# Keeping the running sums of the dense pairs in PSUM, in a four-layer graph network kernel

## The reference, cut to what matters

```
z  = relu(batchnorm2(y2))            # the end of layer 1
x2 = x1 + z                          # residual of layer 1
h  = relu(layernorm(x2))
x3 = x2 + (h after the six steps of layer 2)
g  = relu(layernorm(x3))
out = x3 + tanh(g' @ W1 + b1) @ W2 + b2   # layer 3; likewise without neighbours
```

## Time and profile before

| What | Value |
|---|---|
| median of three runs | 3728.46 us |
| span of the profiled execution, which is its own time here | 3778.5 us |
| PE busy | 2654.6 us, 70% |
| VectorE (DVE) busy | 2151.6 us, 57% |
| ScalarE (ACT) busy | 2009.2 us, 53% |
| GpSimd (POOL) busy | 1431.0 us, 38% |
| mean granted TensorE clock | 0.826 |

### The profile page before, as it was taken

The page is one execution under the profiler, slowest core; times in us unless marked ns, Lnnn a source line. Parts: engine busy times, 40 slices in busy tenths (PEclk is TensorE's granted clock), DMA queues, the critical chain, the costliest instruction groups (busy, mean ns, idle before and its releaser), DMA issues. The chain is left out here.

```text
span 3778.5 us, 45814 instructions
## 1 busy us (share of the span) xinstructions
PE 2654.6 (70%) x11055; PEld 1615.7 (43%) x11055; DVE 2151.6 (57%) x7980; ACT 2009.2 (53%) x4381; POOL 1431.0 (38%) x1507
## 2 busy tenths in 40 slices
PE   4666555656666667799999747787787878775641
PEld 2433333434544545554444322454454545443420
DVE  5533254556658856433333466677677777776620
ACT  1555455556556665455555488565666566553400
POOL 5444434442534335100000000546464645444476
PEclk8877777778888888999999858888889888876865
DMA  4544343344445555334334388444454444333210
GB/s 87 148 132 125 103 119 100 95 121 124 123 128 177 165 150 168 123 133 137 135 136 136 128 259 291 136 144 143 133 160 137 152 143 153 120 106 101 82 58 37
DMA packets 528965, 504.90 MB, mean 134 GB/s; under 512 B 58706, under 2 KB 389955, under 8 KB 528616
## 3 DMA queue, kind: packets, MB, share of 16 engines
q1 hardware_dynamic: 477388, 415.73, 34.4%
q0 software_dynamic: 47184, 85.73, 8.7%
q10 hardware_dynamic: 4172, 0.99, 0.1%
HBM read 246.45 MB, written 260.27 MB: 134 GB/s over the span
## 5 line engine op out<-in xcount | busy, mean ns | idle before, releaser
L1839 POOL DMA_INDIRECT h_G<-step_tab,row_i x294 | 282.0, 959 | 470.3 <-DMA step_tab<-l_NR 194.1
L796 PE MATMUL a_PA<-a_H,w 128*128 128x512 f32 x504 | 308.6, 745 | 197.7 <-ACT a_H L960 160.8
L1839 POOL DMA_INDIRECT h_M<-step_tab,row_i x294 | 283.8, 965 | 227.1 <-PE h_P L1944 148.0
L1559 DVE TENSOR_SCALAR b_Y<-b_BP,col 128x512 f32<-128x512 f32 x148 | 109.9, 743 | 354.2 <-PE b_BP L1513 354.2
L1513 PE MATMUL b_BP<-b_Z,w 128*128 128x512 f32 x592 | 266.3, 592 | 0.0
L270 POOL DMA_INDIRECT h_G<-msg_tab,row_i x147 | 142.1, 967 | 318.4 <-PE h_P L306 150.8
L1541 ACT ACTIVATE b_Z<-b_BQ,bn 128x512 f32<-128x512 f32 x148 | 115.0, 777 | 257.2 <-PE b_BQ L1505 256.9
L208 ACT ACTIVATE l_ln_sd<-l_ln_mv,lneps 128x8 f32<-128x8 f32 (+1 forms) x136 | 41.0, 301 | 383.1 <-DVE l_ln_mv L2149 219.6
L2185 DVE TENSOR_TENSOR_SCAN h_T<-keep,h_T,h_P 128x512 f32<-128x512 bf16 x196 | 223.3, 1139 | 35.7 <-issue 18.6
L796 PEld LDWEIGHTS a_PA<-a_H,w 128*128 128x128 f32 x504 | 105.9, 236 | 322.1 <-ACT a_H L960 191.5
L969 ACT ACTIVATE a_H<-a_PA,col 128x512 f32<-128x512 f32 x252 | 163.7, 669 | 140.0 <-PE a_PA L796 87.8
(11 more groups left out here) (384 smaller groups left out, 6730.5 us busy)
## 6 DMA issues: line engine op xcount, KB each, us to landing
b_HI<-hin_tab SPq DMA_DIRECT2D x148, 256.0 KB, 2.8
y_tab<-b_Y SPq DMA_DIRECT2D x148, 256.0 KB, 2.0
l_Y<-y_tab SPq DMA_DIRECT2D x148, 256.0 KB
l_X<-x_tab SPq DMA_DIRECT2D x148, 256.0 KB
x_tab<-a_X SPq DMA_DIRECT2D x112, 256.0 KB
hin_tab<-a_HI SPq DMA_DIRECT2D x112, 256.0 KB
a_XR<-in_x SPq DMA_DIRECT2D x97, 256.0 KB
out_rows<-l_O SPq DMA_DIRECT2D x97, 256.0 KB
```

What stands on the lines that cost most here:

```text
L796: nc.tensor.matmul(PA[b][:, 0:nt * P], w[:, :], h[b][:, 0:nt, :].rearrange("p t d -> p (t d)"), start=True, stop=True).then_inc(done, 1)
L1559: nc.vector.tensor_scalar(Y[b][:, :], BP[b][:, :], col[:, C_B12:C_B12 + 1], None, ALU.add).then_inc(b_y, 1)
L1839: pool.indirect_dma_start(out=GR_[i % 2][b][:, k, :], out_offset=None, in_=table[:, :], in_offset=bass.IndirectOffsetOnAxis(ap=row_i[:, t ...
```

## The change

For dense pairs the sum stays in the bank XB from the first transpose to the output. `turn` opens the group there with its transposes; a new `add_x1` has PE multiply the loaded x1 rows with the identity matrix onto the transposed z, in one 128x512 float32 matmul for each of the two groups; `x3` and `rows` no longer clear the bank, so r6, h, b2 and the last product land on top. Both layer norms of a dense pair, statistics on DVE and application on ACT, now read the bank. DVE's two adds of a group (in `x2` and `stats2`) are gone, and `rows_out` is a copy. SP's load of the x1 rows two pairs later waits for PE's `add_x1` in place of DVE's add. Edge pairs are as before.

```diff
@@ SP, load_x1
-                        after(sp, x2_set, 2 * (j - 2) + b + 1)
+                        if j >= 2:
+                            sp.wait_ge(*x2_done(j - 2, b))
@@ PE, turn
-                        last = nc.tensor.transpose(turned_in(j, b)[:, k * P:(k + 1) * P], Y[j % 2][b][:, k, :], ident[:, :])
+                        if is_d(j):
+                            last = nc.tensor.matmul(XB[j % 2][b][:, k * P:(k + 1) * P], Y[j % 2][b][:, k, :], ident[:, :], start=(k == 0),
+                                                    stop=(k == 3), is_transpose=True)
+                        else:
+                            last = nc.tensor.transpose(turned_in(j, b)[:, k * P:(k + 1) * P], Y[j % 2][b][:, k, :], ident[:, :])
+            def add_x1(j):
+                for b in range(2):
+                    pe.wait_ge(x1_in[j % 2][b], 16 * (j // 2 + 1))
+                    nc.tensor.matmul(XB[j % 2][b][:, :], ident[:, :], X1[j % 2][b][:, :, :].rearrange("p t d -> p (t d)"), start=False,
+                                     stop=True, skip_group_check=True).then_inc(x2_bank, 1)
@@ PE, the slots
                     turn(j)
+                    if is_d(j):
+                        add_x1(j)
@@ ACT, norm1 and norm2
-                        ln1.act_apply(act, j, b, X2[j % 2][b], NR[j % 2][b])
+                        ln1.act_apply(act, j, b, rows2(j, b), NR[j % 2][b])
-                        rows = X2[j % 2][b][:, k, :] if is_d(j) else XB[j % 2][b][:, k * D:(k + 1) * D]
+                        rows = XB[j % 2][b][:, k * D:(k + 1) * D]
@@ DVE, x2
+                    if is_d(j):
+                        continue
                 for b in range(2):
-                    dve.wait_ge(x2_set, 2 * j + b + 1)
+                    dve.wait_ge(*x2_done(j, b))
@@ DVE, stats2
-                    if is_d(j):
-                        nc.vector.tensor_tensor(X2[j % 2][b][:, :, :], X2[j % 2][b][:, :, :],
-                                                XB[j % 2][b][:, :].rearrange("p (t d) -> p t d", d=D), ALU.add).then_inc(x3_set, 1)
-                for b in range(2):
-                    if is_d(j):
-                        dve.wait_ge(x3_set, 2 * (j - D0) + b + 1)
@@ DVE, rows_out
-                    nc.vector.tensor_tensor(O[b][:, :, :], X2[r][b][:, :, :], XB[r][b][:, :].rearrange("p (t d) -> p t d", d=D),
-                                            ALU.add).then_inc(o_set, 1)
+                    nc.vector.tensor_copy(O[b][:, :, :].rearrange("p t d -> p (t d)"), XB[r][b][:, :]).then_inc(o_set, 1)
```

More of the change, by code:

```diff
@@ L1688, in build @@
     y_in, x1_in = ([sems(f"{n}{r}_", 2) for r in range(2)] for n in ("y_in", "x1_in"))
-    z_set, turned, x2_set, x3_sum, turned2, h_set, p1_set, tanh_set, p2_set, o_set, x3_set = (sem(n) for n in (
-        "z_set", "turned", "x2_set", "x3_sum", "turned2", "ht_set", "p1_set", "tanh_set", "p2_set", "o_set", "x3_set"))
+    z_set, turned, x2_set, x3_sum, turned2, h_set, p1_set, tanh_set, p2_set, o_set, x2_bank = (sem(n) for n in (
+        "z_set", "turned", "x2_set", "x3_sum", "turned2", "ht_set", "p1_set", "tanh_set", "p2_set", "o_set", "x2_bank"))
     normed2 = sems("normed2_", 2)
@@ L1705, in o_stores, with x2_done @@
         return 16 * no2(j, b)
+    def x2_done(j, b):
+        return (x2_bank, 2 * (j - D0) + b + 1) if is_d(j) else (x2_set, 2 * j + b + 1)
     def rows2(j, b):
+        if is_d(j):
+            return _Bank(XB[j % 2][b])
         return X2[j % 2][b] if full(j, b) else _Rows(XS, 4 * group(j, b))
@@ L1903, in x3 @@
                             pe.wait_ge(normed2[b], no2(j - 2, b) + 1)
-                        nc.tensor.matmul(XB[r][b][:, :], ones3[:, :], split_r6[:, :], start=True, stop=False)
+                        nc.tensor.matmul(XB[r][b][:, :], ones3[:, :], split_r6[:, :], start=not is_d(j), stop=False, skip_group_check=is_d(j))
                         if not is_d(j):
@@ L1907, in x3 @@
                         nc.tensor.matmul(XB[r][b][:, :], ident[:, :], NR[r][b][:, :, :].rearrange("p t d -> p (t d)"), start=False,
-                                         stop=True).then_inc(x3_sum, 1)
+                                         stop=True, skip_group_check=is_d(j)).then_inc(x3_sum, 1)
             def turn2(j):
@@ L1928, in rows @@
                     pc_user[b] = (tanh_set, n + 1)
-                    nc.tensor.matmul(XB[j % 2][b][:, :], ones3[:, :], split_out[:, :], start=True, stop=False)
+                    nc.tensor.matmul(XB[j % 2][b][:, :], ones3[:, :], split_out[:, :], start=False, stop=False, skip_group_check=True)
                     for k in range(4):
-                        last = nc.tensor.matmul(XB[j % 2][b][:, k * P:(k + 1) * P], HT[b][:, k, :], w32[:, :], start=False, stop=(k == 3))
+                        last = nc.tensor.matmul(XB[j % 2][b][:, k * P:(k + 1) * P], HT[b][:, k, :], w32[:, :], start=False, stop=(k == 3), skip_group_check=True)
                     last.then_inc(p2_set, 1)
@@ L2115, in x2 @@
                     if full(j, b):
-                        if j >= 2 and is_d(j - 2):
-                            dve.wait_ge(o_set, 2 * (j - 2 - D0) + b + 1)
-                        elif j >= 2 and full(j - 2, b):
+                        if j >= 2 and full(j - 2, b):
                             dve.wait_ge(x3_sum, no2(j - 2, 0) + no2(j - 2, 1) + (b + 1 if j - 2 > MIX else 1))
@@ L2135, in stats2 @@
                         dve.wait_ge(x3_sum, no2(j, 0) + no2(j, 1) + (b + 1 if j > MIX else 1))
-                    if is_d(j):
-                        nc.vector.tensor_tensor(X2[j % 2][b][:, :, :], X2[j % 2][b][:, :, :],
-                                                XB[j % 2][b][:, :].rearrange("p (t d) -> p t d", d=D), ALU.add).then_inc(x3_set, 1)
-                for b in range(2):
-                    if is_d(j):
-                        dve.wait_ge(x3_set, 2 * (j - D0) + b + 1)
                     for k in range(4):
-                        rows = X2[j % 2][b][:, k, :] if is_d(j) else XB[j % 2][b if full(j, b) else 0][:, k * D:(k + 1) * D]
+                        rows = XB[j % 2][b if full(j, b) else 0][:, k * D:(k + 1) * D]
                         last = nc.vector.bn_stats(ln2.st[:, 4 * b + k, :], rows)
@@ L2295, in build, with __init__, __getitem__ @@
     top.close()
+class _Bank:
+    def __init__(self, bank):
+        self.bank = bank
+    def __getitem__(self, at):
+        parts, j, cols = at
+        return self.bank[parts, j * D:(j + 1) * D]
 class _Rows:
```

## The result

The changed kernel takes 3670.27 us (median of 4 runs, 3661.72 to 3683.13), the kernel before 3726.86 (4 runs): a ratio of 0.9848, with a 95% interval of 0.982 to 0.9876. That is 57 us less, where the forecast was 35 (3693 us, range 3668 to 3742); the time is that of the rival "all of it reaches POOL's floor" (3671 us), and outside the forecast's own range of 3676 to 3711.

The account below looks back on a forecast made before the run. The loop through PE, DVE and ACT was taken to bound about half the slots, POOL's round the rest. Slots 18 + boundaries 12 + sixth step and last hops 8 - first pair 2 = 36 us, scaled to 3693 us, range 3668 to 3742.

Parts of the forecast that it names:

- all of it reaches POOL's floor: Rival: filling PE's gap raises its clock, POOL's h_M waits fall to 2.06 us; 58 us gained, 3671 us, chance 0.12.
- DVE's adds are on the path, PE's hole is filled: Slot loop: removing stats2's adds brings statistics, affine and norm2 1.18 us earlier; add_x1 uses PE's 1.84 us wait.
- the clock: PE in the steps: filling its gap may raise PEclk from 0.89, cutting a 3.62 us product to 2.2; only a rival.
- The fill costs 0.2 us a slot and is otherwise free: add_x1 between z's transposes and h_G: 2.2 us of matmuls on PE, h_G turned only 0.2 us later.
- The slots give 18 us, half of them at the floor: Whole steps: 12 of 24 h_M waits above POOL's 2.06 us gain 1.2 us each, 3.6 a step, 18 in five.
- first pair: First dense pair, without a hop or known idle PE to hide add_x1: 2.2 us lost.
- x2's adds are covered by the product, I count them at nothing: DVE's adds in x2, 1.28 us a pair, end before a scan PE needs only after its product; counted as no gain.
- The 8 us given to it: Sixth step and last hops: POOL caps nothing, seven dense pairs remain, six or seven times 1.2 us, 8 us gained.
- Boundaries, 2.4 us each: Between steps, from last h_M batch to next first gather: loop's 1.2 us plus stats2's 1.18, five boundaries, 12 us.
- Statistics and norm from the bank cost nothing: BN_STATS takes 284 ns from PSUM against 280 from SBUF; 32 per pair cost 0.1 us more, counted as nothing.
- The copy: rows_out on DVE as a copy from PSUM: at most 0.1 us a pair longer; taken at the replaced add's time.
- Slower: Rival: add_x1 at low clock takes 3.62 us, above the 3.0 us threshold; 27 us slower, 3755 us, chance 0.17.

Follow-up runs that it names:

- no_add2: Kernel before, with DVE's two adds in stats2 left out for dense pairs and no added PE work: 3233.03 us, ratio 0.9879.
- fill_only: Kernel before plus two float32 identity matmuls per dense pair ahead of z's transposes, results overwritten, DVE's adds kept: 3253.74 us, ratio 0.9943.
- the fourth group: Runs where the kernel before takes 3274 us: changed kernel 3163.3 us, without add_x1's matmuls 3162.98, with a third gather buffer 3154.96.
- after_2: The changed kernel run again, unaltered, in a later group of runs: 3732.7 us, ratio 0.9893 to the kernel before.
- the third group: Runs where the kernel before takes 3774 us, holding the changed kernel again (3732.7 us) and the kernel before without x2's adds (3752.39 us).
- no_add1: Kernel before with DVE's two adds in x2 left out for dense pairs, stats2's adds kept, no added PE work: 3752.39 us, ratio 0.9944.
- fill_double: Changed kernel plus two more identity matmuls per dense pair ahead of z's transposes, results overwritten: 3742.45 us, ratio 0.991 to the kernel before.
- x2_in_x3: Kernel before, x2's adds kept on DVE, stats2's adds replaced by two PE matmuls per pair in x3, behind h_M's turn: 3853.44 us, ratio 1.0222.

## Why the prediction was right, and where its terms were off

**DVE's adds are on the path, PE's hole is filled: right.** The loop named in the prediction (stats2, affine, h_G, norm2) is what got shorter: 43.7 us of idle time ahead of h_G became 2.4, and 66.6 ahead of l_NR became 22.6, while 37.5 came back ahead of the product. no_add2 shows the adds' part, fill_only the filling's, both in the group where the kernel takes 3274 us. The number is partly luck: two terms set at nothing, x2's adds and the clock, were too low, and the measured time lies in the range because that was drawn to take in the rival at 3671.

**The fill costs 0.2 us a slot and is otherwise free: right, and a little too dear.** add_x1 took 1.88 us, not 2.2, and in the fourth group it costs 0.2 us a slot by the two profiles and nothing in the whole kernel. PE's busy time was to rise by 110 us; with the better clock it went from 2654.6 to 2650.7.

**"The slots give 18 us, half of them at the floor": too small.** Of the 24 waits ahead of h_M, 9 stood within 0.2 us of the floor, 14 at 2.5 to 4.1 and one at 6.77; a gain of 1.2 us a slot could take 16 us of the 25 above the floor, by my estimate from POOL's timeline. With x2's adds on the path too (1.2 us more) it would take 23. All 25 went: the waits sum to 47.3 us in the result's profile and to 49.1 in after_2's, from 74.4. Priced by the profiled executions, the five whole steps gave 48.7 us (887.7 to 839.0), where slots, boundaries and first pair were to give 28. What I had only as a rival is the clock: the product's 945 ns became 704, and PEclk 0.88 became 0.96; what this is worth at 3727 or 3774 us no run shows by itself. Nor need all of it be the change's. The profile of before is of an execution 1.3% above the median of its runs, and its like is in the third group (3774 us). Against after_2's profile the five steps give 30.7 us (887.7 to 857.0), steps of 167 to 170 us where 168 to 171 stood, and the kernel 41 us where 36 were summed. So the sum was near for executions like the one it was made from. Scaling it by 3728.46 / 3778.5 changed the 36 us by only 0.5, and the gain isn't proportional: 57 us at 3727, 41 at 3774, 111 at 3274. Why it is 57 and not 41 in the result's group stays open, since no execution of the kernel before near 3727 us was profiled.

**"x2's adds are covered by the product, I count them at nothing": wrong.** Without them alone the kernel is 21 us faster at an unchanged clock. I had looked at one slot, in which the scan's end was not awaited. In no_add1's profile the five steps give 10.2 us (887.7 to 877.5), all of it in the slots. The sixth step with the last hops is 13.6 us shorter (535.3 to 521.7), but that stretch says little: it is 533.0 in after_2, which lacks the same adds, and 522.2 in the result, so single executions differ there by about as much as the adds are worth. The 8 us given to it were too large against after_2 (2.3) and too small against the result (13.1). Which instruction carries the gain of no_add1 was not separated.

**Boundaries, 2.4 us each: between the two profiles.** From 33.85 us in the mean to 30.55 in the result, 3.3 each, which is the rival's 3.4; to 31.9 in after_2, 1.9 each. POOL's waits there went from 25.4 to 21.8 us (101.6 / 4, 87.2 / 4), in after_2 to 23.2.

**Statistics and norm from the bank cost nothing: right.** 281 and 279 ns, and eight parts of norm2 took 2.90 us from the bank for 3.19 from X2 in the slots shown. The rule of the Trainium skill ("Perfetto Trace Analysis", Optimizing Scalar/DVE Operations), 60 ns of access overhead on SBUF against 125 on PSUM, does not show in BN_STATS. The copy, 683 ns, is no test of it, since the add in its place before, 682, read the bank too; that term was right.

**POOL's floor.** For the result its time was the right one, and it was given 0.12. POOL's waits did go to the floor; that POOL's round is what sets the 20.8 us is not shown, since PE waits for no gathered rows there, and only in the fourth group, at about 18 us a slot, does POOL run without a pause. The evidence for a better clock was in the rows, a low one right behind an idle stretch and a product of 3.62 us that could be 2.2; I used it as a rival, and not as a term of the forecast, though fill_only shows it to be worth 0.6% alone, in the groups of 3274 us. "Slower" by 3.0 us of fill is refuted by fill_double, but its price is real elsewhere: x2_in_x3.

## What to carry to other kernels

Moving work to the busiest engine pays where that engine stands waiting at just that place, and two matmuls of the same size a few microseconds later cost more than the whole change gains (x2_in_x3, of whose 121 us x2's adds explain some 21). Place them by the waits of that engine's timeline, not by its busy share. Work that seems covered in one slot has to be looked at in the other slots before it is priced at nothing. And a sum belongs to the execution it is made from: ask first whether the profiled one is like the runs that will be timed, and read a stretch's gain against the spread between executions of the same kernel.

## What the runs showed of the hardware

The same program takes 3274 us or 3727 to 3774. In the long executions DVE and POOL start late on what PE has finished. The changed kernel in the result's group: add_x1, DVE's update before the statistics, then the statistics that read the bank; the second half of the hop's matmuls, then affine:

```profile
2531.65 1.88 PE L1911 MATMUL l_XB<-l_X,ident 128*128 128x512 f32 x4
...
2533.06 1.14 DVE L2224 SCALAR_TENSOR_TENSOR RS<-h_Z,RS 128x512 f32<-128x512 f32 x2
...
2536.23 1.68 DVE L193 BATCH_NORM_STATS2 l_ln_st<-l_XB 128x6 f32<-128x128 f32 x8 [2.02 <-remote]
...
2541.61 0.94 PE L1975 MATMUL h_P<-wht,h_T 128*128 128x128 f32 x6
...
2543.68 0.56 DVE L2203 TENSOR_TENSOR h_Z<-h_P,inv_cnt 128x384 f32<-128x384 f32 x1 [1.53 <-PE h_P L1975]
```

The same kernel in the fourth group:

```profile
2206.74 1.88 PE L1911 MATMUL l_XB<-l_X,ident 128*128 128x512 f32 x4
...
2207.80 1.75 DVE L193 BATCH_NORM_STATS2 l_ln_st<-l_XB 128x6 f32<-128x128 f32 x8
...
2214.10 0.94 PE L1975 MATMUL h_P<-wht,h_T 128*128 128x128 f32 x6
...
2215.07 0.56 DVE L2203 TENSOR_TENSOR h_Z<-h_P,inv_cnt 128x384 f32<-128x384 f32 x1 [0.44 <-PE h_P L1975]
```

Affine follows the last hop matmul by 0.03 us in the fourth group (2215.04 to 2215.07) and by 1.13 in the result's (2542.55 to 2543.68). In the fourth group the statistics start 1.06 us after add_x1 begins, when its first half is in. In the result's they start 4.58 us after; until 2534.20 DVE was at the update, and then it stood 2.02 us, 2.70 past the end of add_x1. Ends of matmuls are modelled, so the delay may lie in PE or in the signal. The floor of about 2 us ahead of POOL's h_M batches, which the prediction took as given, may be of this kind: in the fourth group it is 0.30. The third and fourth groups ran on one chip, so it isn't the chip; what brings the delay is open.
